# Window attention and displaced blur: one-piece read of x1, a row of ones in the blur product, and several steps moved in the hand-written order

## What is computed

```
def gn(v):                       # 32 groups of 6 channels, over the whole image
    return (v - mean) / sqrt(var + 1e-5)

# window attention: 7 x 7 windows, 12 heads of 16 channels
qkv  = einsum('bchw,oc->bohw', gn(x), w_qkv)        # then cut into windows
dots = einsum('wnid,wnjd->wnij', q, k) * 16 ** -0.5 + bias_table[rel_index]
out  = einsum('wnij,wnjd->wnid', softmax(dots), v)
x1   = x + einsum('bchw,oc->bohw', out, w_proj) + b_proj

# displaced blur: 8 positions of 24 channels; each channel is shifted by a
# rounded offset (zeros outside) and convolved with a normalized 5 x 5 Gaussian
y    = x1 + depthwise_conv(displace(gn(x1), offset), kernel)
```

## Time and profile before

| | |
|---|---|
| runs | 6381.01, 6397.56, 6429.35 us; median 6397.56 |
| profiled execution | 6416.5 us; span of the trace 6414.7 us |
| mean granted TensorE clock | 0.893 of 2.4 GHz |
| busy | PE 5579.4 us (87%), DVE 4304.0 (67%), ACT 3830.3 (60%), POOL 3961.2 (62%) |
| DMA | 790.17 MB, 1,371,147 packets, of which 1,184,840 under 512 bytes |

### The profile page before, as it was taken

The page is one execution under the profiler, slowest core; times in us unless marked ns, Lnnn a source line. Parts: engine busy times, 40 slices in busy tenths (PEclk is TensorE's granted clock), DMA queues, the critical chain, the costliest instruction groups (busy, mean ns, idle before and its releaser), DMA issues. The chain is left out here.

```text
span 6414.7 us, 256829 instructions
## 1 busy us (share of the span) xinstructions
PE 5579.4 (87%) x97860; PEld 4640.6 (72%) x97860; DVE 4304.0 (67%) x9677; ACT 3830.3 (60%) x8451; POOL 3961.2 (62%) x4452
## 2 busy tenths in 40 slices
PE   5998888888888888888888889888898888988895
PEld 4777777777777777777777777777777777777774
DVE  4666666676676666666766766766666666766663
ACT  2665656665566656666665666665666655666562
POOL 1566556666567665666665566665566656666665
PEclk9888988998899988889998899999899889899986
DMA  3455565555654555655565655565555556545553
GB/s 82 107 129 128 125 132 121 121 124 131 132 126 115 127 129 123 135 122 118 130 134 127 130 122 123 128 134 131 128 125 123 123 130 134 129 117 125 128 115 68
DMA packets 1371147, 790.17 MB, mean 123 GB/s; under 512 B 1184840, under 2 KB 1234312, under 8 KB 1365768
## 3 DMA queue, kind: packets, MB, share of 16 engines
q1 hardware_dynamic: 1369992, 773.90, 54.9%
HBM read 156.97 MB, written 154.14 MB: 48 GB/s over the span
## 5 line engine op out<-in xcount | busy, mean ns | idle before, releaser
L1185 POOL TENSOR_TENSOR probl<-prob,probh 98x588 f16<-98x588 f32 x1024 | 1349.2, 1318 | 349.4 <-DVE probh L1029 250.2
L1191 POOL TENSOR_TENSOR o<-osb,o 128x192 f16<-128x192 f32 x1024 | 601.0, 587 | 1449.9 <-ACT o L830 1418.0
L629 PE MATMUL pO<-vv,probh 98*49 98x34 f16 x24576 | 1019.9, 224 | 74.0 <-issue 59.9
L629 PEld LDWEIGHTS pO<-vv,probh 98*49 98x49 f16 x24576 | 868.7, 122 | 248.6 <-issue 223.1
L629 PE MATMUL pO<-vv,probl 98*49 98x34 f16 x12288 | 989.2, 228 | 2.0 <-issue 2.0
L822 ACT ACTIVATE mov<-pT 12x98 f16<-12x98 f32 x1024 | 247.8, 242 | 999.5 <-PE pT L596 996.4
L1014 DVE TENSOR_REDUCE mx<-pS 128x12 f32<-128x588 f32 x1024 | 778.1, 760 | 33.9 <-issue 16.1
L614 PE MATMUL pT<-qst,kst 96*98 96x49 f16 x12288 | 776.5, 210 | 25.6 <-issue 25.6
L817 ACT ACTIVATE prob<-pT 98x588 f32<-98x588 f32 x1024 | 673.1, 657 | 188.0 <-PE pT L614 180.8
L629 PEld LDWEIGHTS pO<-vv,probl 98*49 98x49 f16 x12288 | 774.9, 122 | 0.0
L1029 DVE CAST probh<-prob 98x588 f16<-98x588 f32 x1024 | 600.6, 587 | 225.6 <-ACT prob L817 208.3
(11 more groups left out here) (184 smaller groups left out, 16645.6 us busy)
## 6 DMA issues: line engine op xcount, KB each, us to landing
kst<-kh SPq DMA_DIRECT2D x1536, 98.0 KB, 2.2
qst<-qh SPq DMA_DIRECT2D x1536, 49.0 KB, 2.0
qst<-mix SPq DMA_DIRECT2D x768, 98.0 KB, 2.6
kst<-mix SPq DMA_DIRECT2D x768, 98.0 KB, 2.2
vv<-cv SPq DMA_DIRECT2D x1024, 73.5 KB
xr<-x_scratch SPq DMA_DIRECT2D x128, 588.0 KB
out<-xr SPq DMA_DIRECT2D x256, 294.0 KB
x_scratch<-xm SPq DMA_DIRECT2D x128, 392.0 KB, 3.2
```

The lines of the kernel that those rows point to most:

```text
L629: mm = pe.matmul(pO[64 * win:64 * win + NT, OW * hp:OW * hp + OW], b[0:98, p % 2, PW * hp + NT * win:PW * hp + NT * win + NT], vv[:, g % 2 ...
L1185: pool.tensor_tensor(probl[0:98, p % 2, :], prob[0:98, p % 2, :], probh[0:98, p % 2, :], ALU.subtract).then_inc(S["pl_p"], 1)
L1191: pool.tensor_tensor(o16[:, p % 2, C:2 * C], osb[:, p % 2, :], o16[:, p % 2, 0:C], ALU.subtract).then_inc(S["ol_p"], 1)
```

## The change

1. **x1 through DRAM.** The scratch tensor is laid out as (parity, row, channel, column), as `xr` wants it. `store_x1` has four DMAs in place of two, which write runs of 56 floats; `read_x1` is one DMA of 112 long rows in place of four of short runs.
2. **Row of ones.** `xr`, `xcf`, `xc`, `coef` and `amat` get two partitions more (114). `xr` has ones there, `coef` the offset of the normalization, and `amat` the sums of its rows of each parity: the blur product adds the offset itself, and POOL's addition (L1228) and its semaphore go. Setup gets two matmuls with the new constant `ext`, after the gather of the bias and before `amat`, and a memset. The product that makes `coef` takes four matmuls in place of two.
3. **pX** moves from the bank of `pT` to that of `pO`. `shifted` no longer waits for `ox_a`; `attend` does, and the transposes wait for `on_d` of the pair attended in the same step.
4. **TensorE's order** becomes: attend, scores, turn, blur stage 0, q k, turn_out, shifted, blur stage 1, values, projection. On ScalarE `turned_out` moves to the end of the step.
5. **Steps.** Projection comes a step later, in odd steps (4r+7, and 4r+9 for the tail), values in even steps, six pairs ahead; so SP spreads values with p % 4 = 1. The second normalization, the last store, the read, and all of the blur come a step later.
6. **Tail bn_stats**: one each in steps 27, 31, 3 and 5 in place of four in step 4.

```diff
-LEAD = 5
+LEAD = 6
...
-            if p % 2 and (att if p + LEAD < PAIRS else nxt):
+            if p % 2 == 0 and (att if p + LEAD < PAIRS else nxt):
...
-                    s = PPR * r + 6 + (LATE_TAIL if tail and r < NWX - 1 else 0)
+                    s = PPR * r + 7 + (LATE_TAIL if tail and r < NWX - 1 else 0)
...
-        pX = pT[:, 0, 320:512].bitcast(F16).rearrange("p (b t) -> p b t", b=3)
+        pX = pO[:, 320:512].bitcast(F16).rearrange("p (b t) -> p b t", b=3)
...
-                sp.dma_start(scratch[0:CM, t], xm[:, par(i), t]).then_inc(S["x1_out"], 16)
-                sp.dma_start(scratch[CM:C, t], xt[64 * h:64 * h + 64, par(i), CHUNK * (k % 2):CHUNK * (k % 2) + CHUNK]
-                             ).then_inc(S["x1_out"], 16)
-
-            def read_x1(y0, y1):
-
-                v = scratch.rearrange("(c s) (y x) -> s y c x", s=2, x=HW)
+                y = slice(2 * WS * k, 2 * WS * k + 2 * WS)
                 for s in (0, 1):
-                    sp.dma_start(xr[HW * s + y0:HW * s + y1, :].rearrange("y (c x) -> y c x", x=HW),
-                                 v[s][y0:y1]).then_inc(S["xr_in"], 16)
+                    sp.dma_start(scratch[s, y, 0:CM // 2].rearrange("y c x -> c y x"),
+                                 xm[s::2, par(i), t].rearrange("c (y x) -> c y x", x=HW)).then_inc(S["x1_out"], 16)
+                    sp.dma_start(scratch[s, y, CM // 2:CC].rearrange("y c x -> c y x"),
+                                 xt[64 * h + s:64 * h + 64:2, par(i), CHUNK * (k % 2):CHUNK * (k % 2) + CHUNK]
+                                 .rearrange("c (y x) -> c y x", x=HW)).then_inc(S["x1_out"], 16)
+
+            def read_x1():
+
+                sp.dma_start(xr[0:SY, :], scratch.rearrange("s y c x -> (s y) (c x)")).then_inc(S["xr_in"], 16)
...
-                    v = before(v_step, p, prev, att, nxt) if p % PPR == 2 else None
+                    v = before(v_step, p, prev, att, nxt) if p % PPR == 1 else None
...
-                    if p == 4 and prev:
+                    if p == 5 and prev:
                         store_x1(i - 1, NCH - 1)
-                    if p == 5 and prev:
+                    if p == 6 and prev:
...
-                        read_x1(0, HW // 2)
+                        read_x1()
...
+            pe.wait_ge(S["setup"], SET_EXT)
+            for n, bank in enumerate((pV, pQ)):
+                mm = pe.matmul(bank[0:SX, 0:POS * HW], const("ext", SY),
+                               xr[0:SY, (2 + n) * POS * HW:(3 + n) * POS * HW], start=True, stop=True,
+                               skip_group_check=True)
             mm.then_inc(S["setup_pe"], 1)
...
-                if due("ox_a", i, p - 2):
-                    pe.wait_ge(S["ox_a"], nth("ox_a", i, p - 2))
                 for hp in range(NHP):
                     bank, at = hp // 3, PW * (hp % 3)
                     pe.matmul(pT[0:98, bank, at:at + PW], biasT[:, PW * hp:PW * hp + PW], mov[:, :],
...
                 if due("on_d", i, p):
                     pe.wait_ge(S["on_d"], nth("on_d", i, p))
+                if due("ox_a", i, p - 1):
+                    pe.wait_ge(S["ox_a"], nth("ox_a", i, p - 1))
...
-                    for n, q in at(p, 3, prev, att, nxt):
-                        turn_out(i + n, q)
-                    b = blur_step(p, 13, prev)
+                    b = blur_step(p, 14, prev)
                     if b is not None:
                         blur(i - 1, b, 0)
-                    v = v_step(p, att, nxt)
...
-                    if v:
-                        values(i + v[0], v[1])
                     if nxt and p == 14:
                         pe.wait_ge(S["gn1_dve"], nth("gn1_dve", i + 1, 7))
                     q = qk_step(p, att, nxt)
                     if q:
                         qk(i + q[0], q[1], q[2])
+                    for n, q in at(p, 2, prev, att, nxt):
+                        pe.wait_ge(S["on_d"], nth("on_d", i + n, q + 1))
+                    for n, q in at(p, 3, prev, att, nxt):
+                        turn_out(i + n, q)
                     if att:
                         shifted(i, p)
                     if b is not None:
                         blur(i - 1, b, 1)
+                    v = v_step(p, att, nxt)
...
+                    if v:
+                        values(i + v[0], v[1])
...
-                    if prev and p == 4:
-                        dve.wait_ge(S["x1_p"], nth("x1_p", i - 1, 16))
-                        for t in range(4):
+                    for n, t, on in ((0, 0, att and p == 27), (0, 1, att and p == 31), (-1, 2, prev and p == 3),
+                                     (-1, 3, prev and p == 5)):
+                        if on:
+                            dve.wait_ge(S["x1_p"], nth("x1_p", i + n, 2 * (t + 4) + 2))
                             dve.bn_stats(gst[1][:, 8 + t, :],
-                                         xt[:, par(i - 1), ROW * t:ROW * t + ROW]).then_inc(S["gn2_bn"], 1)
+                                         xt[:, par(i + n), ROW * t:ROW * t + ROW]).then_inc(S["gn2_bn"], 1)
...
-                        pool.tensor_tensor(v, src, spread(coef[:, 0, cols], HW), ALU.mult).then_inc(S["xcm_p"], 1)
-                        pool.wait_ge(S["xcm_p"], nth("xcm_p", i - 1, b + 1))
-                        pool.tensor_tensor(v, v, spread(coef[:, 1, cols], HW), ALU.add).then_inc(S["xcf_p"], 1)
+                        pool.tensor_tensor(v, src, spread(coef[:, cols], HW), ALU.mult).then_inc(S["xcf_p"], 1)
```

More of the change, by code:

```diff
@@ L201, in build @@
         gnb = sb("gnb", [128, 2], F32)
-        coef = sb("coef", [SY, 2, CC], F32)
+        coef = sb("coef", [SX, CC], F32)
         cmain, ctail = (xcf[0:n, b, 0:n].rearrange("p (a c) -> p a c", a=2)
@@ L668, in blur @@
                     src = z
-                m = 2 * (b // (CPP // 2 // BC)) + (1 if stage == 0 else 0)
+                m, n = 2 * (b // (CPP // 2 // BC)) + (1 if stage == 0 else 0), SX if stage == 0 else SY
                 for j in range(BC // 2):
                     k = slice(SY * j, SY * j + SY)
-                    mm = three(pM[0:SY, k], src[:, b % 2, 0, k], src[:, b % 2, 1, k],
-                               amat[:, 0, m, :], amat[:, 1, m, :])
+                    mm = three(pM[0:SY, k], src[0:n, b % 2, 0, k], src[0:n, b % 2, 1, k],
+                               amat[0:n, 0, m, :], amat[0:n, 1, m, :])
                 mm.then_inc(S["c1_pe" if stage == 0 else "c2_pe"], 1)
@@ L684, in body @@
                         turn(i, p)
+                    b = blur_step(p, 14, prev)
+                    if b is not None:
+                        blur(i - 1, b, 0)
+                    if nxt and p == 14:
+                        pe.wait_ge(S["gn1_dve"], nth("gn1_dve", i + 1, 7))
+                    q = qk_step(p, att, nxt)
+                    if q:
+                        qk(i + q[0], q[1], q[2])
+                    for n, q in at(p, 2, prev, att, nxt):
+                        pe.wait_ge(S["on_d"], nth("on_d", i + n, q + 1))
                     for n, q in at(p, 3, prev, att, nxt):
                         turn_out(i + n, q)
-                    b = blur_step(p, 13, prev)
+                    if att:
+                        shifted(i, p)
                     if b is not None:
-                        blur(i - 1, b, 0)
+                        blur(i - 1, b, 1)
                     v = v_step(p, att, nxt)
@@ L953, in _ @@
             then(dve.tensor_tensor(gauss, gauss, spread(inside, HW), ALU.mult))
-            for s in (0, 1):
-                v = slice(HW * s, HW * s + HW)
-                m = const("smask", SY)[:, s:s + 1]
-                then(dve.tensor_scalar(amat[:, 0, :, v], gauss, m, None, ALU.mult))
-                then(dve.scalar_tensor_tensor(out=amat[:, 1, :, v], in0=gauss, scalar=m,
-                                              in1=amat[:, 0, :, v], op0=ALU.mult, op1=ALU.subtract))
+            assert count[0] == SET_EXT, count
+            dve.wait_ge(S["setup_pe"], 2)
+            for n, bank in enumerate((pV, pQ)):
+                ext = bank[0:SX, 0:POS * HW].rearrange("p (a y) -> p a y", y=HW)
+                k = slice(POS * n, POS * n + POS)
+                for s in (0, 1):
+                    v = slice(HW * s, HW * s + HW)
+                    m = const("smask", SX)[:, s:s + 1]
+                    then(dve.tensor_scalar(amat[:, 0, k, v], ext, m, None, ALU.mult))
+                    then(dve.scalar_tensor_tensor(out=amat[:, 1, k, v], in0=ext, scalar=m,
+                                                  in1=amat[:, 0, k, v], op0=ALU.mult, op1=ALU.subtract))
+            then(dve.memset(xr[96:SX, :], 1.0))
             then(dve.memset(pO[:, :], 1.0))
@@ L1076, in body @@
                         maximum(i, p)
-                    if prev and p == 5:
+                    if prev and p == 6:
                         aggregate(1, i - 1)
```

110 lines of the change are left out of this document (51 added, 59 removed).

## The result

Before: median 6404.65 us of 4 runs (6381.01 to 6429.35). After: median 6178.2 us of 4 runs (6168.64 to 6202.82). The ratio is 0.9652, interval 0.9604 to 0.97: faster by 226 us, where 386 were forecast. The profiled execution took 6184.96 us, its span is 6183.1.

The account below looks back on a forecast made before the run. The prediction found no engine full overall, with TensorE or POOL binding some stretches and waits others. Its terms gave -12.5 us per image over 31 bodies, with setup and last body -386, so 6012 us, range 5830 to 6260.

Parts of the forecast that it names:

- R2: Rival: the read of x1, or something else instead, is late; -7.5 us per image, 6167 us; chance 13%.
- A: Steps 11 to 13: the new path of x1 makes its read timely; -7 us per image, between -9 and -2.
- ceiling 23.66 - 14.72: Most that steps 11 to 13 could gain, priced by steps 8 to 10: 8.9 us per image.
- B: Steps 4 to 7: spread tail bn_stats and moved pX remove waits; -5 us per image, between -7.6 and -2.
- 1.33 us of POOL lateness is mostly covered: Steps 4 to 7: transposes, moved after the q, k product, would mostly stop waiting 1.33 us for POOL.
- C: Blur, mainly steps 19 to 22: row of ones replaces POOL's addition; -3.5 us per image, between -5 and -2.
- D: Moved values product and transposes lose cover and add waits on TensorE; +2.7 us per image, between -1 and +6.
- R3: Rival: the on_d wait puts normalize, transposes and shifted in series every step; slower, sum up to +17 per image; chance 5%.
- E: SP's extra DMAs taken as even; short writes meet at the loop's edge; +0.3 us per image, between 0 and +2.
- Setup: Before the loop: amat must wait for TensorE's ext product behind the bias gather; +10 us, between +5 and +14.
- Last body: End of the program: shorter wait for the x1 read, less 1 us for the short-run store; -8 us.
- R4: Rival: gaps go but TensorE's low clock moves to other steps; -4.8 us per image, 6250 us; chance 15%.

Follow-up runs that it names:

- e1: The kernel before with only the new path of x1 through DRAM (short runs in the store, one read of long rows): 6318.51 us, ratio 0.9857.
- e2: The kernel after with the old path of x1 (stores in long rows, read in four DMAs of short runs): 6165.13 us, ratio 0.9615.
- e7b: The kernel after, reading one channel of x1 in place of 96, with zeros for the others and the row of ones: 6037.61 us, ratio 0.9449.
- e5: The kernel after with the four tail bn_stats together again, in step 5: 6215.92 us, ratio 0.9701.
- e4: The kernel after with POOL repeating the normalization's multiplication in each blur step, into an unread spare tile: 6262.56 us, ratio 0.9779.
- e3: The kernel after with the values product back ahead of the q, k product in TensorE's order, still in even steps: 6068.83 us, ratio 0.9457.
- e9: The kernel after with ScalarE's om copy (turned_out) ahead of its q, k copies in the step: 6321.95 us, ratio 0.9856.
- e6: The kernel after with six extra matmuls into an unused PSUM bank in each of steps 12 and 13: 6058.31 us, ratio 0.9469.

## Why the prediction came out as it did

The sign and the range held; the forecast of 6012 us was 166 too low. The time is R2's (6167) by luck: R2 has the read late or something else late in its place, and the read was in time in all bodies but the last (coef was late by 14.9 us in the whole run). Nor did the sum hold by its terms. A pass is 7.4 us shorter where 12.5 were forecast, and the terms that fell short and the 3.66 us that nobody had counted are partly made up by a gain that wasn't counted either (1.85 in 29 to 31). By its own steps:

**A (-7): the mechanism right, the size wrong.** The wait for the read went, and with it part of what TensorE waited for, 2.7 us per image (e1). The step that failed is "ceiling 23.66 - 14.72": it priced 11 to 13 by a stretch at clock 1.00, and the clock of 11 to 13 didn't rise with the wait gone. Beside the other parts the new path is worth nothing at all (e2): a blur one step later had already given the old read its time in all but 14 images.

**Left out: what the read does to others.** This term stood at nothing, without a reason. The read's bytes are on the queues in steps 7 to 9, and there TensorE stood for its own instructions: 8 to 10 grew by 3.66, and e7b puts the whole cost of the read there at 4.66. I had the row of 0.98 queue share in front of me and asked only whether the read would be in time, not who else is on the queues. In the kernel before, that stretch was full too and yet fast: the instruction queue has packets in it there as well (60 begin in it in 30 passes, 80 after), but `issue` took 0.9 us per pass where it takes 3.4 now. Why TensorE stands for them so much longer isn't settled.

**B (-5): measured -3.10 in 4 to 7.** The tails are 1.75 of it there and 1.2 for the whole pass (e5). Almost all of the gain is busy time, the clock going from 0.70 to 0.82; the idle time of the stretch went only from 4.2 to 3.9 us. What failed is "1.33 us of POOL lateness is mostly covered": in step 5 the transposes wait for POOL's out_lo in every pass, 51.6 us in 30 or 1.7 each.

**C (-3.5): -2.7** (e4), within its bounds; 19 to 22 went from 25.70 to 23.46. POOL's busy time fell by 360 us, not 390: out_lo takes 621 ns now, 587 before.

**D (+2.7): +3.5** for the place of values alone (e3, 109 us over 31 bodies), where I had 1.2 + 0.4 for it: within the bounds of D, but twice its own part. I looked for it in a wait of 0.6 us, and 2.1 us of it are TensorE's busy time at the lower clock in the steps that lost their cover. The on_d wait is far from R3's, but 44.4 us in the run for osb are 1.4 per image where I had 0.4, nearly all in step 12. The q, k product's wait for xnt grew from 108.7 to 152.3 us, 1.4 per image where I had 0.7, most of it in step 22, which I hadn't listed. What I didn't count is attend's wait for om, 140.8 us; what it costs is open, since e9 removed it only by a worse order.

**E (+0.3): 29 to 31 took 1.85 less**; TensorE's stand at the loop's back edge (15.55 us with 11.67 busy in the earlier trace rows) is gone, 10.74 with 8.84 now, and the 59.9 us of `issue` there with it. They are nearly gone in e2 as well (4.6 us) and stay in e1 (57.1), so it isn't the new path; which of the moves did it wasn't tried.

**Setup (+10): +14.6**, just beyond its bound of +14. **Last body (-8): -3.9.**

**R4 (15%) was the mechanism that I underrated.** The low clock of 12 to 14 is the new schedule's: 20.90 us at 0.85 before, 23.38 at 0.64 after, and 0.64 with the old read too (e2), 0.80 with the new path alone (e1). e6 shows what it is worth, 120 us, by giving TensorE work there. With the read's cost in 8 to 10 (141 us, e7b) these are two losses of some 4 us per image each, where the forecast missed by 5. No run removes both, so whether they add up isn't shown.

## What to carry to other kernels

Don't price the removal of a wait by a stretch with the clock at 1.00 unless something in the change raises the clock: here the wait went and the clock stayed (e1), and it rose when the light steps had more work (e6). Before making a transfer earlier, denser or longer, list everything on the queues in those microseconds, the engines' own instructions and the next image's load among it. Compare queue shares as times, share times span, when the spans differ. When steps are moved, look at what the lightest steps are left with: the values product had a second use as their filling.

## What was not expected of the hardware

- TensorE stands up to 3.7 us in the middle of a loop pass, with its inputs ready, while the data queues are 84 to 93% busy, and goes on 1.3 to 1.8 us after a packet of the instruction queue; with the queues at 47% it doesn't stand (75.1 us against 0.6 in the run). Full queues alone don't do it: with the short-run read (e2) it is 40.8 us.
- Twelve more matmuls of 392 columns per image shorten three steps from 23.38 to 19.19 us, the granted clock going from 0.63 to 1.00 in the windows shown (2.4 GHz throughout) and from 0.64 to 0.96 over the 30 passes. Ahead of the fall, in the pass shown, TensorE was busy for 15.89 of 19.54 us, and then had steps of attention with little beside it.
- A read of 2.4 MB in rows of 5.4 KB or 21.5 KB holds others up alike (71.0 and 75.1 us).
- With 10,752 runs of 224 bytes per image in the writes and long rows in the read, the queues are full for 4.1 us less per image than the other way round (e2 against the kernel after).
